# A graph-attention kernel: the first graph's scores taken straight from K and Q

## The chip, the cores and the metric

One core of one Trainium2 chip. The metric is the device time of one execution in microseconds (us), median of several executions.

## The reference

For each of 32 graphs of 256 nodes with 256 features (8 heads of 32), in float32:

```
q, k, v = x @ Wq.T + bq, x @ Wk.T + bk, x @ Wv.T + bv      # split into 8 heads of 32
scores  = q @ k.T * 32**-0.5 * (adj + adj)                 # per head, 256 x 256
attn    = softmax(scores, axis=-1)
ctx     = attn @ v                                         # heads side by side: 256 x 256
out     = layernorm(x + ctx @ Wo.T + bo)
```

## The kernel before

Graphs are worked on singly, but K and Q are projected for a pair of graphs at once (two graphs' 512 nodes are the columns). Every engine runs a loop written out by hand, `step(g)` for g from -4 to 34, with eight places o = 0..7 in it, and does its part of several graphs in a fixed order; semaphores join them. A place o of step g turns head o of graph g (`turn_probs`) and makes the scores three heads ahead (`rows`); three projections of K and Q for a coming pair, the projection of V for the next graph, and the output projection are laid between.

To keep float32 precision with one-pass matmuls, an operand is cut into a high part (rounded) and a low part (the rest), in the type F32R. For the scores, K's and Q's parts of one head, 32 features each, are stacked on 128 rows: four groups of 32 rows hold K high, low, high, low against Q high, high, low, low. So one matmul of 128 rows adds all four products. The way to such a stack is long:

- TensorE projects (`project_kq`, L240; pair 0 uses four banks, later pairs share `proj_bank`, so each projection waits until ScalarE has read the one before);
- ScalarE reads the bank into `whole` and adds the bias (`read_kq`, L477; semaphore `kq_out`);
- GpSimd cuts it into `parts` (`cut_kq`, L538 and L540; `kq_low`);
- 32 copies of 32 x 1024 elements each build `stack` (for K and Q, four pairs of heads, four groups). For all pairs but the first, these are DMAs issued by SyncE (L192), after the DMA that loads the transposed x of the pair after (`xt`, L184, one buffer). For pair 0, SyncE issues 12 of them (K, pairs of heads 0 to 2), VectorE makes 12 and ScalarE 8 by copies (`stack_first`, L145).

VectorE multiplies the scores by the mask `adj_rows` and takes the row maximum in one instruction (`reduce_rows`, L341), ScalarE makes the exponentials (`exp`, L447), TensorE transposes them (L223), VectorE (one head in eight: ScalarE) moves them out, and they multiply V (`weigh_v`, L278). `turn_shares` (L266) spreads the reciprocals of the sums. ScalarE's `cut_x` (L469) takes the high part of `xt`, GpSimd's `low_x` (L546) the low part (`xt_low`). `copy_v` (L481) moves V out. ScalarE also issues the loads of the masks and of x (`load_masks`, `load_x`).

The order of ScalarE around the change, by place: in step -1 `read_kq(1, 0)` at 1, `copy_v(0)` at 3, `read_kq(1, 1)` at 5, `exp(0, 0)` at 7; in step 0 `exp(0, 1)` at 0, `load_masks(1)` and `read_kq(1, 2)` at 1, `load_x(0)` at 2, `copy_v(1)` at 3, then at 4 `exp(0, 5)`, `move_turned`, `cut_x(2, 0)`, at 5 `exp(0, 6)`, `read_kq(1, 3)`, `cut_x(2, 1)`, at 6 `exp(0, 7)`, and at 7 `exp(1, 0)`.

Of the kernel before, what the change touches and what calls it, by code (L numbers as in the profile page):

```python
# [40 lines left out]
def build(nc, x, x_t, adj, adj_t, wq, wk, wv, wo, bq, bk, bv, bo, out):  # L41
    ctx = ExitStack()
    with ctx:
# [83 lines left out]
        def kq_bank(pair, c):  # L127

            return (*row_bank, *turn_bank)[c] if pair == 0 else proj_bank
# [7 lines left out]
            else:  # L137
                wait(eng, moved_dve, (H - len(ON_ACT)) * g + o + 1 - sum(n < o for n in ON_ACT))

        def stack_first(eng, copy, which, j):  # L140

            eng.wait_ge(kq_low, 2 * which + 2)
            for group in range(J):
                part = group % 2 if which == 0 else group // 2
                copy(stack[D * group:D * (group + 1), 0, which, j, :],  # L145
                     parts[D * j:D * (j + 1), 2 * which + part, :]).then_inc(stacked[0][which][j], 16)

        def run_steps(step):
            for g in range(-4, B + 3):
# [2 lines left out]
        def is_graph(g):  # L152
            return 0 <= g < B
# [12 lines left out]
        @block.sync  # L166
        def _(sp):
            sp.dma_start(xt[:].rearrange("p t s -> p (t s)"), x_t[0]).then_inc(xt_in, 16)
            for n, dram in enumerate((wk, wq, wv, wo)):
                sp.dma_start(w_whole[:, n], dram).then_inc(weight_in[n], 16)  # L170
                if n == 0:
                    for tile, bias_dram in ((b_k, bk), (b_q, bq)):
                        sp.dma_start(tile[:], bias_dram).then_inc(biases_in, 16)
            for tile, dram in ((b_v, bv), (b_o, bo)):
                sp.dma_start(tile[:], dram).then_inc(biases_in, 16)

            def step(g):
                if g % 2 == 0 or not is_pair(g + 3):
                    return
                pair = (g + 3) // 2  # L180
                if g + 5 < 2 * PAIRS:

                    wait(sp, xt_low, 2 * pair + 2)
                    sp.dma_start(xt[:].rearrange("p t s -> p (t s)"), x_t[pair + 1]).then_inc(xt_in, 16)  # L184
                for which in range(1 if g == -3 else 2):
                    wait(sp, kq_low, 4 * pair + 2 * which + 2)
                    for j in range(J - 1 if g == -3 else J):

                        wait(sp, rows_made, 8 * g + 2 * j + 2)
                        for group in range(J):  # L190
                            part = group % 2 if which == 0 else group // 2
                            sp.dma_start(stack[D * group:D * (group + 1), pair % 2, which, j, :].bitcast(F32),  # L192
                                         parts[D * j:D * (j + 1), 2 * which + part, :].bitcast(F32)
                                         ).then_inc(stacked[pair % 2][which][j], 16)

            run_steps(step)

        @block.tensor
        def _(pe):
            def rows(n, o):  # L200
                if o % T == 0:
                    for which in range(2):
                        pe.wait_ge(stacked[(n // 2) % 2][which][o // T],
                                   (n // 4) * (J * 16) + J * 16)

                wait(pe, rows_used, 8 * n + o - 1)
                if n == 0 and o == 0:
                    pe.wait_ge(kq_out, 4)
                q, key = head(n // 2, 1, o, n % 2), head(n // 2, 0, o, n % 2)
                for t in range(T):  # L210
                    last = nc.tensor.matmul(row_bank[o % 2][:, t * S:(t + 1) * S], q[:, t * P:(t + 1) * P], key,  # L211
                                            start=(t == 0), stop=True, skip_group_check=True)
                last.then_inc(rows_made, 1)
# [89 lines left out]
                last.then_inc(bias_made, 1)  # L303

            def step(g):
                if g == -2:
                    make_bias()
                for o in range(H):
                    if is_graph(g):
                        turn_probs(g, o)  # L310
                    if o < 5 and is_graph(g):
                        rows(g, o + 3)
                    if o >= 5 and is_graph(g + 1):
                        rows(g + 1, o - 5)
                    if (g % 2, o) in KQ_SLOTS:
                        ahead = kq_ahead(g, o, KQ_SLOTS)
                        if is_pair(g + ahead):
                            project_kq((g + ahead) // 2, *KQ_SLOTS[g % 2, o])
                    if o == 1 and is_graph(g - 1):
                        turn_shares(g - 1, 1)  # L320
                        weigh_v(g - 1, 1)
                    if o == 2 and is_graph(g + 1):
                        project_v(g + 1)
                    if o == 5 and is_graph(g):
                        turn_shares(g, 0)
                        weigh_v(g, 0)
                    if o == 6 and is_graph(g - 1):
                        project_out(g - 1)
# [4 lines left out]
        def _(dve):  # L333
# [56 lines left out]
            for n in range(4):  # L390
# [4 lines left out]
                dve.wait_ge(w_high, n + 1)  # L395
                nc.vector.tensor_tensor(w_parts[:, 1, n].rearrange("p t e -> p (t e)"), tile, high.bitcast(F32),
                                        ALU.subtract).then_inc(w_cut, 1)
            dve.wait_ge(bias_made, 1)
            nc.vector.tensor_copy(bias[:], out_bank[:, 0:E]).then_inc(bias_ready, 1)
            for which, j in ((0, 3), (1, 0), (1, 2)):  # L400
                stack_first(dve, nc.vector.tensor_copy, which, j)

            def step(g):
                for o in range(H):
# [7 lines left out]
                        lower_top(g, o + 2)  # L412
                    if o >= 6 and is_graph(g + 1):
                        lower_top(g + 1, o - 6)
                    if o == 0 and is_graph(g - 1):
                        divide(g - 1, 1)
                    if o in (0, 1) and is_graph(g - 2):
# [15 lines left out]
        def _(act):  # L433
# [37 lines left out]
            def read_kq(pair, c):  # L471
# [2 lines left out]
                if pair == 0 and c == 0:  # L474
                    act.wait_ge(biases_in, 4 * 16)
                b = (b_k if c < 2 else b_q)[:, c % 2:c % 2 + 1]
                nc.scalar.activation(whole[:, c % 2, :], kq_bank(pair, c)[:], ACT.Identity, bias=b).then_inc(kq_out, 1)  # L477

            def copy_v(n):
                act.wait_ge(v_made, n + 1)  # L480
# [11 lines left out]
            nc.scalar.preload_act_table_set("natural_log_exp_and_others")  # L492

            def step(g):
                for o in range(H):
                    if g == -2 and o == 6:
                        stack_first(act, nc.scalar.copy, 1, 1)
                        stack_first(act, nc.scalar.copy, 1, 3)
                    if o < 7 and is_graph(g):
                        exp(g, o + 1)  # L500
                    if o == 7 and is_graph(g + 1):
                        exp(g + 1, 0)
                    if is_graph(g) and o in ON_ACT:
                        move_turned(g, o)
# [24 lines left out]
        def _(pool):  # L529
            def cut_kq(pair, c):  # L530
                cut = slice((c % 2) * 512, (c % 2 + 1) * 512)
                pool.wait_ge(kq_out, 4 * pair + c + 1)
                if c % 2 == 0:

                    if pair > 0:
                        for j in range(J):
                            pool.wait_ge(stacked[(pair - 1) % 2][c // 2][j], ((pair - 1) // 2 + 1) * (J * 16))
                nc.gpsimd.tensor_copy(parts[:, 2 * (c // 2), cut], whole[:, c % 2, :]).then_inc(kq_high, 1)  # L538
                pool.wait_ge(kq_high, 4 * pair + c + 1)
                nc.gpsimd.tensor_tensor(parts[:, 2 * (c // 2) + 1, cut], whole[:, c % 2, :],  # L540
                                        parts[:, 2 * (c // 2), cut].bitcast(F32),
                                        ALU.subtract).then_inc(kq_low, 1)

# [116 lines left out]
```

## Time and profile before

| | us |
|---|---|
| median of 3 executions | 520.39 (519.92 to 523.06) |
| the profiled execution | 522.89 |
| its span, first to last instruction | 521.1 |
| TensorE (PE) busy in it | 472.7, at a mean granted clock of 0.974 |
| VectorE (DVE) busy | 429.8 |
| ScalarE (ACT) busy | 384.0 |
| GpSimd (POOL) busy | 348.7 |

Busy time is the sum over an engine's instructions. The profiled execution carries 1.8 us outside its span. Times in the rows below count from the span's start.

### The profile page before, as it was taken

What the parts mean: (1) busy time and instruction counts of PE and PEld (TensorE: products, weight loads), DVE (VectorE), ACT (ScalarE), POOL (GpSimd) and SP (SyncE); (2) the same over time, 40 slices, a digit from 0 to 9 for tenths busy, and PEclk for the clock granted to TensorE, in tenths of its full rate; (3) what the DMA queues carried; (4) which work ended last, traced back from release to release, by engine and by line L of the source; (5) the groups of instructions that cost most, each with busy time, mean ns of one, the idle gap of its engine ahead of it and who ended that gap; (6) DMA issues with size and microseconds to landing.
All of it is one profiled execution on the core that took longest, in us unless ns stands there. A gap on an engine that the chain in (4) does not pass through costs nothing.

```text
span 521.1 us, 15227 instructions
## 1 busy us (share of the span) xinstructions
PE 472.7 (91%) x4742; PEld 395.2 (76%) x4742; DVE 429.8 (82%) x1815; ACT 384.0 (74%) x1257; POOL 348.7 (67%) x518
## 2 busy tenths in 40 slices
PE   4569999999999999999999999999999999998872
PEld 3357887878788788878888787878888787877752
DVE  4547888888888898888888998988889888888881
ACT  2478887777878777787878777787878777777750
POOL 4724557686876767696876767786776768664444
PEclk9859999999999999999999999999999999999996
DMA  5709897988889798898889897998989889795101
GB/s 161 173 29 240 207 222 176 233 202 205 227 208 240 173 254 193 218 219 206 227 202 235 199 244 173 230 219 205 231 187 260 187 220 214 165 246 128 61 23 41
DMA packets 40322, 100.11 MB, mean 192 GB/s; under 512 B 9649, under 2 KB 17842, under 8 KB 40242
## 3 DMA queue, kind: packets, MB, share of 16 engines
q1 hardware_dynamic: 26930, 73.96, 60.8%
q10 hardware_dynamic: 13312, 25.17, 16.8%
q8 instruction: 39, 0.64, 0.6%
q14 instruction: 41, 0.34, 0.2%
HBM read 26.22 MB, written 8.39 MB: 66 GB/s over the span
## 4 chain that ended last, share of the span: by engine, by line
PE 65%; POOL 21%; issue 5%; DVE 4%; ACT 3%; DMA 1%; POOLq 0%; DVEq 0%; SPq 0%; ACTq 0%
PE turn_bank L223 17%; PE proj_bank L240 11%; PE v_bank L253 9%; PE row_bank L211 8%; PE ctx_bank L278 8%; POOL xt_parts L546 7%; PE ctx_bank L266 5%; PE out_bank L290 5%; POOL parts L540 4%; POOL result L586 3%; POOL ctx_parts L554 2%; POOL scale L573 2%; POOL parts L538 2%; ACT probs L447 2%; POOL ctx_parts L552 1%
## 5 line engine op out<-in xcount | busy, mean ns | idle before, releaser
L447 ACT ACTIVATE probs<-probs,low_top 128x256 f32<-128x256 f32 x512 | 257.6, 505 | 100.9 <-DVE low_top L349 98.4
L356 DVE COPY turned_probs<-turn_bank 128x512 f32<-128x512 f32 x224 | 154.7, 691 | 53.7 <-PE turn_bank L223 52.9
L341 DVE CUSTOM_DVE_ANT_0 probs<-row_bank,adj_rows 128x256 f32<-128x256 f32 x512 | 192.2, 414 | 6.1 <-PE row_bank L211 6.1
L223 PE MATMUL turn_bank<-ident,probs 128*128 128x128 f32 x1024 | 158.2, 277 | 7.8 <-ACT probs L447 7.7
L223 PEld LDWEIGHTS turn_bank<-ident,probs 128*128 128x128 f32 x1024 | 119.5, 141 | 52.1 <-ACT probs L447 23.4
L240 PE MATMUL proj_bank<-xt_parts,w_parts 128*128 128x512 f32 x360 | 107.0, 407 | 21.4 <-POOL xt_parts L546 16.2
L211 PE MATMUL row_bank<-stack 128*128 128x256 f32 x512 | 124.3, 325 | 0.7 <-DVE top L341 0.7
L447 ACT ACTIVATION_READ_ACCUMULATOR probs<-probs,low_top 128x1 f32 x512 | 97.3, 190 | 0.0
L540 POOL TENSOR_TENSOR parts<-whole,parts 128x512 fp32r<-128x512 f32 x64 | 82.9, 1296 | 5.3
L240 PEld LDWEIGHTS proj_bank<-xt_parts,w_parts 128*128 128x128 f32 x360 | 61.0, 193 | 30.8 <-POOL xt_parts L546 19.2
L552 POOL CAST ctx_parts<-context 128x256 fp32r<-128x256 f32 x64 | 25.5, 398 | 86.0 <-DVE context L366 86.0
L211 PEld LDWEIGHTS row_bank<-stack 128*128 128x128 f32 x512 | 78.2, 193 | 1.1 <-issue 0.9
L538 POOL CAST parts<-whole 128x512 fp32r<-128x512 f32 x64 | 39.6, 619 | 50.8 <-ACT whole L477 50.8
L278 PE MATMUL ctx_bank<-turned_probs,v 128*32 128x256 f32 x1024 | 67.0, 379 | 0.0
L290 PE MATMUL out_bank<-w_parts,ctx_parts 128*128 128x256 f32 x384 | 51.7, 285 | 2.2 <-POOL ctx_parts L554 2.2
L253 PE MATMUL v_bank<-w_parts,xt_parts 128*128 128x256 f32 x384 | 52.2, 286 | 0.0
L554 POOL TENSOR_TENSOR ctx_parts<-context,ctx_parts 128x256 fp32r<-128x256 f32 x64 | 47.1, 736 | 5.1
L290 PEld LDWEIGHTS out_bank<-w_parts,ctx_parts 128*128 128x128 f32 x384 | 48.4, 192 | 2.7 <-POOL ctx_parts L554 2.7
L253 PEld LDWEIGHTS v_bank<-w_parts,xt_parts 128*128 128x128 f32 x384 | 49.3, 195 | 0.2
L546 POOL TENSOR_TENSOR xt_parts<-xt,xt_parts 128x512 fp32r<-128x512 f32 x32 | 41.9, 1311 | 7.0 <-ACT xt_parts L469 7.0
L341 DVE DVE_READ_ACCUMULATOR2_ANT top<- 128x1 f32 x512 | 43.4, 85 | 0.0
L266 PE MATMUL ctx_bank<-ident,shares 128*32 128x128 f32 x1024 | 41.2, 278 | 1.6 <-DVE shares L361 1.5
(44 smaller groups left out, 473.0 us busy)
## 6 DMA issues: line engine op xcount, KB each, us to landing
stack<-parts SPq DMA_DIRECT2D x492, 128.0 KB, 2.6
xt<-in_x_t SPq DMA_DIRECT2D x16, 512.0 KB, 3.9
adj_rows<-in_adj ACTq DMA_DIRECT2D x16, 512.0 KB, 4.7
xr<-in_x ACTq DMA_DIRECT2D x16, 512.0 KB, 7.5
out<-result ACTq DMA_DIRECT2D x32, 256.0 KB, 3.2
turned_probs<-in_wk SPq DMA_DIRECT2D x1, 256.0 KB, 4.0
turned_probs<-in_wq SPq DMA_DIRECT2D x1, 256.0 KB, 3.8
turned_probs<-in_wv SPq DMA_DIRECT2D x1, 256.0 KB, 4.0
```

Source lines behind the costliest of these rows:

```text
L211: last = nc.tensor.matmul(row_bank[o % 2][:, t * S:(t + 1) * S], q[:, t * P:(t + 1) * P], key, start=(t == 0), stop=True, skip_group_check ...
L223: last = nc.tensor.transpose(turn_bank[o % 2][:, c * S + t * P:c * S + (t + 1) * P], probs[:, o % RING, t * S + c * P:t * S + (c + 1) * P] ...
L240: last = nc.tensor.matmul(kq_bank(pair, c)[:], w_parts[:, a, c // 2, t, features], xt_parts[:, pair % 2, b, t, :], start=(half_ == 0 and n ...
L253: last = nc.tensor.matmul(v_bank[:, tile * E:(tile + 1) * E], xt_parts[:, (n // 2) % 2, a, t, nodes], w_parts[:, c, 2, t, :], start=(tile ...
L266: nc.tensor.matmul(ctx_bank[c:c + D, S + t * P:S + (t + 1) * P], shares[:, g % 2, o, t:t + 1].to_broadcast([P, D]), ident[:], start=True, ...
L278: last = nc.tensor.matmul(ctx_bank[c:c + D, 0:S], v[:, (g // 2) % 2, g % 2, t, o * D:(o + 1) * D], turned_probs[:, o, t * S:(t + 1) * S], ...
L290: last = nc.tensor.matmul(out_bank[:, n * E:(n + 1) * E], ctx_parts[:, g % 2, a, f, nodes], w_parts[:, b, 3, f, :], start=(n == 0 and i == 0),
L341: last = nc.vector.tensor_tensor_reduce(probs[:, o % RING, t * S:(t + 1) * S], row_bank[o % 2][:, t * S:(t + 1) * S], adj_rows[:, (n // 2) ...
L356: nc.vector.tensor_copy(turned_probs[:, o, :], turn_bank[o % 2][:]).then_inc(moved_dve, 1)
L447: last = nc.scalar.activation(tile, tile, ACT.Exp, bias=low_top[:, n % 2, o, t:t + 1], accum_out=sums[:, n % 2, o, t:t + 1])
L540: nc.gpsimd.tensor_tensor(parts[:, 2 * (c // 2) + 1, cut], whole[:, c % 2, :], parts[:, 2 * (c // 2), cut].bitcast(F32), ALU.subtract).the ...
L546: nc.gpsimd.tensor_tensor(xt_parts[:, pair % 2, 1, t, :], xt[:, t, :], xt_parts[:, pair % 2, 0, t, :].bitcast(F32), ALU.subtract).then_inc ...
```

## The change

Graph 0's scores are no longer made from the stacks, but from K and Q as ScalarE read them out, in float32, each head on its own 32 rows of the array (`rows_of_first`, with `tile_position`). For pair 0 the readouts go to `y` and `result`, which nothing else uses yet (`read_out`), in place of `whole`. Graph 1 still uses pair 0's stacks. All 32 of these are now issued by SyncE; VectorE and ScalarE copy none. TensorE makes graph 0's first three heads of scores at the start of step -1 instead of in its places 5 to 7, followed by the product for the bias (`make_bias`, before at the start of step -2); VectorE copies the bias out at the end of step -1; ScalarE makes the first exponential at the start of step -1 instead of its end.

```diff
--- before.py
+++ after.py
@@ -137,13 +137,11 @@
             else:
                 wait(eng, moved_dve, (H - len(ON_ACT)) * g + o + 1 - sum(n < o for n in ON_ACT))
 
-        def stack_first(eng, copy, which, j):
-
-            eng.wait_ge(kq_low, 2 * which + 2)
-            for group in range(J):
-                part = group % 2 if which == 0 else group // 2
-                copy(stack[D * group:D * (group + 1), 0, which, j, :],
-                     parts[D * j:D * (j + 1), 2 * which + part, :]).then_inc(stacked[0][which][j], 16)
+        def read_out(pair, c):
+
+            if pair == 0:
+                return (y, result)[c // 2][:, c % 2].rearrange("p t e -> p (t e)")
+            return whole[:, c % 2, :]
 
         def run_steps(step):
             for g in range(-4, B + 3):
@@ -182,9 +180,9 @@
 
                     wait(sp, xt_low, 2 * pair + 2)
                     sp.dma_start(xt[:].rearrange("p t s -> p (t s)"), x_t[pair + 1]).then_inc(xt_in, 16)
-                for which in range(1 if g == -3 else 2):
+                for which in range(2):
                     wait(sp, kq_low, 4 * pair + 2 * which + 2)
-                    for j in range(J - 1 if g == -3 else J):
+                    for j in range(J):
 
                         wait(sp, rows_made, 8 * g + 2 * j + 2)
                         for group in range(J):
@@ -197,15 +195,29 @@
 
         @block.tensor
         def _(pe):
+            def rows_of_first(o):
+
+                wait(pe, rows_used, o - 1)
+                if o == 0:
+                    pe.wait_ge(kq_out, 4)
+                j, f = o // T, o % T
+                own = slice(D * j, D * (j + 1))
+                q, key = read_out(0, 2 + f), read_out(0, f)
+                for t in range(T):
+                    last = nc.tensor.matmul(row_bank[o % 2][:, t * S:(t + 1) * S], q[own, t * P:(t + 1) * P], key[own, 0:S],
+                                            start=(t == 0), stop=True, tile_position=(D * j, 0), skip_group_check=True)
+                last.then_inc(rows_made, 1)
+
             def rows(n, o):
+                if n == 0:
+                    rows_of_first(o)
+                    return
                 if o % T == 0:
                     for which in range(2):
                         pe.wait_ge(stacked[(n // 2) % 2][which][o // T],
                                    (n // 4) * (J * 16) + J * 16)
 
                 wait(pe, rows_used, 8 * n + o - 1)
-                if n == 0 and o == 0:
-                    pe.wait_ge(kq_out, 4)
                 q, key = head(n // 2, 1, o, n % 2), head(n // 2, 0, o, n % 2)
                 for t in range(T):
                     last = nc.tensor.matmul(row_bank[o % 2][:, t * S:(t + 1) * S], q[:, t * P:(t + 1) * P], key,
@@ -303,14 +315,16 @@
                 last.then_inc(bias_made, 1)
 
             def step(g):
-                if g == -2:
+                if g == -1:
+                    for o in range(3):
+                        rows(0, o)
                     make_bias()
                 for o in range(H):
                     if is_graph(g):
                         turn_probs(g, o)
                     if o < 5 and is_graph(g):
                         rows(g, o + 3)
-                    if o >= 5 and is_graph(g + 1):
+                    if o >= 5 and 0 < g + 1 < B:
                         rows(g + 1, o - 5)
                     if (g % 2, o) in KQ_SLOTS:
                         ahead = kq_ahead(g, o, KQ_SLOTS)
@@ -395,10 +409,6 @@
                 dve.wait_ge(w_high, n + 1)
                 nc.vector.tensor_tensor(w_parts[:, 1, n].rearrange("p t e -> p (t e)"), tile, high.bitcast(F32),
                                         ALU.subtract).then_inc(w_cut, 1)
-            dve.wait_ge(bias_made, 1)
-            nc.vector.tensor_copy(bias[:], out_bank[:, 0:E]).then_inc(bias_ready, 1)
-            for which, j in ((0, 3), (1, 0), (1, 2)):
-                stack_first(dve, nc.vector.tensor_copy, which, j)
 
             def step(g):
                 for o in range(H):
@@ -412,6 +422,9 @@
                         lower_top(g, o + 2)
                     if o >= 6 and is_graph(g + 1):
                         lower_top(g + 1, o - 6)
+                    if g == -1 and o == 7:
+                        dve.wait_ge(bias_made, 1)
+                        nc.vector.tensor_copy(bias[:], out_bank[:, 0:E]).then_inc(bias_ready, 1)
                     if o == 0 and is_graph(g - 1):
                         divide(g - 1, 1)
                     if o in (0, 1) and is_graph(g - 2):
@@ -474,7 +487,7 @@
                 if pair == 0 and c == 0:
                     act.wait_ge(biases_in, 4 * 16)
                 b = (b_k if c < 2 else b_q)[:, c % 2:c % 2 + 1]
-                nc.scalar.activation(whole[:, c % 2, :], kq_bank(pair, c)[:], ACT.Identity, bias=b).then_inc(kq_out, 1)
+                nc.scalar.activation(read_out(pair, c), kq_bank(pair, c)[:], ACT.Identity, bias=b).then_inc(kq_out, 1)
 
             def copy_v(n):
                 act.wait_ge(v_made, n + 1)
@@ -492,13 +505,12 @@
             nc.scalar.preload_act_table_set("natural_log_exp_and_others")
 
             def step(g):
+                if g == -1:
+                    exp(0, 0)
                 for o in range(H):
-                    if g == -2 and o == 6:
-                        stack_first(act, nc.scalar.copy, 1, 1)
-                        stack_first(act, nc.scalar.copy, 1, 3)
                     if o < 7 and is_graph(g):
                         exp(g, o + 1)
-                    if o == 7 and is_graph(g + 1):
+                    if o == 7 and 0 < g + 1 < B:
                         exp(g + 1, 0)
                     if is_graph(g) and o in ON_ACT:
                         move_turned(g, o)
@@ -535,9 +547,9 @@
                     if pair > 0:
                         for j in range(J):
                             pool.wait_ge(stacked[(pair - 1) % 2][c // 2][j], ((pair - 1) // 2 + 1) * (J * 16))
-                nc.gpsimd.tensor_copy(parts[:, 2 * (c // 2), cut], whole[:, c % 2, :]).then_inc(kq_high, 1)
+                nc.gpsimd.tensor_copy(parts[:, 2 * (c // 2), cut], read_out(pair, c)).then_inc(kq_high, 1)
                 pool.wait_ge(kq_high, 4 * pair + c + 1)
-                nc.gpsimd.tensor_tensor(parts[:, 2 * (c // 2) + 1, cut], whole[:, c % 2, :],
+                nc.gpsimd.tensor_tensor(parts[:, 2 * (c // 2) + 1, cut], read_out(pair, c),
                                         parts[:, 2 * (c // 2), cut].bitcast(F32),
                                         ALU.subtract).then_inc(kq_low, 1)
 
```

## Rows read from the trace of the kernel before

**Rows 1.** Page, busy time by engine: us, share of the span, instructions

```profile
PE 472.7 (91%) x4742; PEld 395.2 (76%) x4742; DVE 429.8 (82%) x1815; ACT 384.0 (74%) x1257; POOL 348.7 (67%) x518
```

**Rows 2.** Windows of one us: engines, granted clock (PEclk), DMA share

```profile
core 0: us, PE busy (x) PEld busy (x) DVE busy (x) ACT busy (x) POOL busy (x), PEclk, DMA share, GB/s
23.00:24.00 1.00, 0.00 (x0) 0.00 (x0) 0.87 (x1) 0.89 (x1) 1.00 (x2) 0.65 0.88 193
...
40.00:41.00 1.00, 1.00 (x6) 0.77 (x6) 1.00 (x5) 0.44 (x2) 0.00 (x0) 0.82 0.98 213
```

**Rows 3.** Timeline of PE, 17 to 72 us: start, length, what

```profile
18.74 0.96 PE L240 MATMUL proj_bank<-xt_parts,w_parts 128*128 128x512 f32 x3 [1.29 <-ACT xt_parts L469]
24.30 1.65 PE L240 MATMUL proj_bank<-xt_parts,w_parts 128*128 128x512 f32 x3 [4.60 <-POOL xt_parts L546]
25.74 2.76 PE L253 MATMUL v_bank<-w_parts,xt_parts 128*128 128x256 f32 x12
32.40 2.93 PE L240 MATMUL proj_bank<-xt_parts,w_parts 128*128 128x512 f32 x6 [3.90 <-ACT whole L477]
...
38.68 1.05 PE L223 MATMUL turn_bank<-ident,probs 128*128 128x128 f32 x4
...
51.96 0.60 PE L223 MATMUL turn_bank<-ident,probs 128*128 128x128 f32 x4
...
61.24 0.48 PE L211 MATMUL row_bank<-stack 128*128 128x256 f32 x2
```

**Rows 4.** Timeline of ACT, 17 to 72 us

```profile
17.49 0.69 ACT L477 ACTIVATE whole<-turn_bank,b_q 128x512 f32<-128x512 f32 x1 [0.16 <-PE turn_bank L240]
...
23.11 8.52 ACT L145 CAST stack<-parts 32x1024 fp32r<-32x1024 f32 x8 [4.43 <-POOL parts L540]
31.66 0.69 ACT L477 ACTIVATE whole<-proj_bank,b_k 128x512 f32<-128x512 f32 x1
...
46.78 0.62 ACT L469 CAST xt_parts<-xt 128x512 fp32r<-128x512 f32 x1
...
50.63 0.52 ACT L447 ACTIVATE probs<-probs,low_top 128x256 f32<-128x256 f32 x1
```

**Rows 5.** Timeline of SP: DMA issues

```profile
15.66 7.57 SPq L192 DMA_DIRECT2D stack<-parts  x12
24.27 0.33 SPq L184 DMA_DIRECT2D xt<-in_x_t  x1
...
38.13 10.54 SPq L192 DMA_DIRECT2D stack<-parts  x16
...
51.02 10.82 SPq L192 DMA_DIRECT2D stack<-parts  x16
```

**Rows 6.** DMA view, windows 40 to 42, 42 to 44, 46 to 49.5 us: KB, us to landing

```profile
adj_rows<-in_adj ACTq DMA_DIRECT2D x1, 512.0 KB, 4.5
...
xr<-in_x ACTq DMA_DIRECT2D x1, 512.0 KB, 7.0
...
stack<-parts SPq DMA_DIRECT2D x4, 128.0 KB, 6.1
```

**Rows 7.** Everything on tile xt: landing of its loads

```profile
DMA to landing us min/median/max: 3.3/3.9/6.2
```

**Rows 8.** Chain of work: start, us on the chain, what

```profile
14.34 1.06 PE out_bank L301 x4
...
54.39 0.24 PE row_bank L211 x2
...
55.20 0.86 PE ctx_bank L278 x16
56.06 0.59 PE turn_bank L223 x4
...
58.31 0.44 PE turn_bank L223 x4
...
58.99 0.69 PE proj_bank L240 x3
```

## Prediction

> **What bounds the kernel now.** I read the busy times first: TensorE is busy 91% of the span [rows 1], so over the 32 graphs it sets the pace, and the kernel's time is the moment at which graph 0 gets under way plus a train of steps that no part of this change touches. Any gain is a shift of that train. I therefore read the start, engine by engine. The end of it is best seen where TensorE transposes the first head of a graph: graph 0's at 38.68 us and graph 1's at 51.96 [rows 3].
>
> What holds graph 0 back: TensorE's work for step -2 ends at 19.70 (18.74 + 0.96), and its next projection waits for the low part of x until 24.30. Then V, until 28.5, and then nothing until 32.40 [rows 3]. The next projection needs `proj_bank` read by ScalarE, and ScalarE copies stacks from 23.11 to 31.63, and reads the bank at 31.66 [rows 4]. Because TensorE idled from 19.70, its granted clock fell between 23 and 24 us and came back only between 40 and 41 [rows 2]: the work of 24.3 to 40.4 went at 1.2 GHz.
>
> **What the change takes away: the start.** Scores of graph 0 need only K and Q read out. The last readout ends at 18.18 [rows 4], before TensorE is free at 19.70. Price of a head in float32: two tiles, each two instructions of 256 columns. The nearest row is `weigh_v`'s, also float32, 256 columns and on a quarter of the array: 16 instructions, four side by side, in 0.86 us, so 0.215 us each when alone; `make_bias` has 4 in 1.06, 0.265 each [rows 8]. A head is thus 0.86 to 1.06 us; I take 0.86, since the first row has the quarter tiles. A head from the stacks took 0.24 [rows 8]. To that comes the change of tiling: the transposes right after `weigh_v` take 0.59 against 0.44 elsewhere, so 0.15 for each change, 0.30 a head. In sum about 1.15 a head, 0.9 more than before.
>
> The Trainium skill, TensorEngine Tiling, section Key Properties, says that changing the tiling mode drains TensorE; the 0.15 us agrees. The skill's TensorE: Matmul & The Clock Gate, Part 3, says that a weight load overlaps matmuls in flight only when its row group differs, and here both tiles of a head have the same one. No row here shows loads on row tiles. By that rule the loads would add to each head, and the sum would be lower by the price given with the rivals.
>
> Heads 0 and 1 take 19.7 to 21.7, head 2 follows when VectorE has used the first bank (masks were issued early and nothing else waits for VectorE then), then `make_bias`, to about 24.2. TensorE's gap is gone, so I expect the clock to stay at 2.4 GHz. From 24.30, at the full clock's prices: 3 instructions of projection 0.69 [rows 8], V 1.43 (12 of 256 columns; half of the 2.76 in rows 3, and what 12 such take at the full clock), two projections 1.4, to 27.8. ScalarE no longer has copies in the way; its readout is 0.69, then one more projection, 29.2. There graph 0's first transpose starts, against 38.68: 9.5 us earlier. VectorE's bias copy, moved behind a wait, has only step 0's work behind it and ends by 25.
>
> **What it adds in step 0.** Five heads (3 to 7) cost TensorE 0.9 more each. Up to head 6's transpose, TensorE does 6 transposes (2.7), 5 float32 heads (5.75), one stack head 0.24, three projections 2.1, V 1.43, `turn_shares` and `weigh_v` with their change of tiling 1.5: 13.7, so it gets there at 42.9. Before, the same place came at 48.8 (38.68 + 10.1). If nothing else bound, the shift would be 5.9 to 6.1.
>
> **What it adds on SyncE, and what is late next.** SyncE issued 12 copies in 7.57 us from 15.66, and 16 in 10.54 and 10.82 later [rows 5]: 0.63 to 0.68 each. Pair 0 now has 32: 15.66 + 32 x 0.655 = 36.6. The second half needs GpSimd's last cut, which was there at 23.1, when ScalarE's copies began [rows 4], and SyncE comes to it only at 26. Behind these 32 stands SyncE's load of `xt` for pair 2, which it issued at 24.27 [rows 5] and will now issue at 36.7. That load takes 3.3 to 6.2 us to land, median 3.9 [rows 7]. Near it are the loads of masks and x, issued by ScalarE with step 0, now about 30.6 and 32.8: before, these took 4.5 and 7.0 us, and a stack copy issued 6 us after the first of them needed 6.1 [rows 6], with a DMA share of 0.98 at 40 us [rows 2]. `xt` is issued exactly 6 us after the masks' load and behind stack copies in the same queue, so it lands at 40.6 to 44; I take 6.2 after 37.0 (its issue done), 43.2.
>
> Who waits: ScalarE's `cut_x(2, 0)`, and behind it in its order head 6's exponential, the readout of Q, `cut_x(2, 1)`, head 7's exponential and graph 1's first. Before, `cut_x(2, 0)` started at 46.78 with ScalarE busy without a pause from there to graph 1's first exponential at 50.63 [rows 4]; TensorE's first transpose of graph 1 was at 51.96. So from this place on the shift is 46.8 minus the landing: 46.8 - 43.2 = 3.6. The ends: landing at 40.6 gives 6.1 by ScalarE, and TensorE's own chain caps it at about 6; landing at 44.1 gives 2.7.
>
> Graph 1's stacks of the first pair of heads land about 31 and are needed at 40. Graph 2's: K's 16 copies from 37.3 to 47.8, then four of Q's to 50.5, landed by 53 to 55 with the queue as full as at 46 us; needed at 61.24 - 3.6 = 57.6 [rows 3, 5]. Covered by 3 us or more; with a shift of 6 it would be even. Later pairs have SyncE pausing for GpSimd, 48.67 to 51.02 in the rows, and the train keeps its shift. The copies saved on VectorE and ScalarE give nothing more: in steps they have no part.
>
> **Sum.** 522.89 - 3.6 = 519.3 for an execution like the profiled one, whose own time is 2.5 above the median of the three. Applied to the median: 520.39 - 3.6 = 516.8.
>
> **Rivals.**
>
> *No stall on xt.* SyncE's issues or the queue run faster, and TensorE binds in step 0. Shift 5.2 to 6.2, time 514.2 to 515.2. For it: the median landing of 3.9 gives 40.9. Against it: that median is taken mostly with no bulk loads ahead. Chance 0.22.
>
> *The early clock falls all the same*, because quarter-array float32 counts for little or the gaps at 17 to 18.7 and 24 do. Then 24.30 to the last projection goes as in rows 3: V ends at 28.5, two projections 31.4, readout 32.1, projection 33.6; step 0 keeps its old slow start and pays the five heads: 5.1 - 4.5 + some 2 of old waits = 2.6, and `xt` is no longer late. Time 517.8. Chance 0.13.
>
> *Weight loads not hidden.* 4 loads a head at some 0.19 add 0.76, five heads 3.8; TensorE would reach head 6 at 46.7, against 44.9 with the late `xt`. Shift 2.1, time 518.3; chance 0.10.
>
> *Slower than before: the wait takes the clock.* With `xt` late, TensorE sits from 42.9 to some 44.9, waiting for head 6's exponential. Before, an idle TensorE lost its clock 3.6 us or a little more after 19.70 [rows 2, 3]. If the landing is at 45 or later, the pause is as long, and the clock can go until some 17 us later as it did the first time; with TensorE's work dense there, up to 8 us are lost. Shift 1.8 - 8 = -6, time up to 526; if the clock returns in 4 us, the loss is 2 and the shift about 0. Chance of a time above before's 0.07; it decides from a landing at 45.
>
> *It doesn't show*: the shift is eaten again later, by stacks of graph 2 that land late or GpSimd's low part of x: 520.4. Chance 0.05.
>
> **Numbers.** My forecast (late `xt`, shift 2.4 to 5.2) has 0.43. The time is 516.8. The range takes in the rival without stall on its fast side (514.2, and 0.7 for the scatter of the medians) and on the slow side shifts down to about 0: 513.5 to 520.8; what lies outside is the clock lost a second time, and parts of the others. One per cent, 5.2 us, is about what a measurement of this kernel can tell from no change. Faster by more than that: the rival without stall and a little of the forecast, 0.25. Within: 0.70. Slower by over 1%: 0.05.
>
> **What the profile after would show.** Heads 0 and 1 at 19.7 on TensorE, four instructions each, some 0.2 apart; the clock at 1.0 from 20 to 40; ScalarE's readout of pair 1 near 25; the first transpose of graph 0 near 29; 32 copies by SyncE to 36.6 and `xt` behind them, a wait of ScalarE for `xt` of 2 to 4 us near 39 to 43, a TensorE wait of some 2 us before head 6; graph 1's first transpose near 48.4, and from there rows like before's, 3.6 earlier. The forecast is wrong if the float32 heads cost much above 1.15 us, if the clock differs, or if `xt` lands outside 41.6 to 44.4.

## The result and the profile after

The changed kernel is slower by about a third of a per cent: 522.54 us median of 18 executions (520.02 to 524.77) against 520.41 of 18 before, ratio 1.0035 with a 95% interval of 1.0021 to 1.0048. I had forecast 516.8, 3.6 us faster. The profiled execution took 523.15 us, its span 521.3 against 521.1. Before's profiled execution lies 2.5 us above its median and the changed kernel's 0.6, so the two profiles differ by 0.3 us where the medians differ by 2.1.

The busy times [rows 1] changed by what was moved: TensorE more, VectorE and ScalarE less by their copies.

```profile
PE 478.7 (92%) x4758; PEld 398.9 (77%) x4758; DVE 420.2 (81%) x1803; ACT 374.6 (72%) x1249; POOL 346.5 (66%) x518
```

The timeline of TensorE after, to be read against [rows 3]. L207 are the float32 heads, L235 the transposes. In the rows below, the number before the engine's name is how long the row took, and brackets hold how long the engine stood idle before it and for what:

```profile
30.39 0.60 PE L235 MATMUL turn_bank<-ident,probs 128*128 128x128 f32 x4
30.92 1.13 PE L207 MATMUL row_bank<-y,result 32*128 32x256 f32 x4
31.98 0.96 PE L252 MATMUL proj_bank<-xt_parts,w_parts 128*128 128x512 f32 x3
...
43.53 1.05 PE L290 MATMUL ctx_bank<-turned_probs,v 128*32 128x256 f32 x16
47.33 1.11 PE L235 MATMUL turn_bank<-ident,probs 128*128 128x128 f32 x4 [2.75 <-ACT probs L460]
...
52.02 1.05 PE L235 MATMUL turn_bank<-ident,probs 128*128 128x128 f32 x4
```

Graph 0's first transpose comes at 30.39, 8.3 us earlier than before's 38.68. Graph 1's first comes at 52.02, where it was 51.96. The whole lead is lost inside step 0. For head 6 the row of before is this:

```profile
48.83 0.66 PE L223 MATMUL turn_bank<-ident,probs 128*128 128x128 f32 x4
```

TensorE after is done with the work ahead of it at 44.58 (43.53 + 1.05), so 4.2 us of the lead are left there: the float32 heads took 4.0, where the forecast gave them 3.6. Then TensorE stands 2.75 us ahead of head 6, and the stretch behind it takes another 1.6. ScalarE's timeline says what it stands for:

```profile
40.56 0.58 ACT L470 COPY turned_probs<-turn_bank 128x512 f32<-128x512 f32 x1 [0.49 <-PE turn_bank L235]
45.66 0.62 ACT L482 CAST xt_parts<-xt 128x512 fp32r<-128x512 f32 x1 [4.52 <-DMA xt<-in_x_t]
46.18 0.51 ACT L460 ACTIVATE probs<-probs,low_top 128x256 f32<-128x256 f32 x1
```

It waits 4.52 us for `xt`. SyncE's timeline, and the DMA view of a window at the load's issue (KB, us to landing):

```profile
16.01 21.02 SPq L190 DMA_DIRECT2D stack<-parts  x32
37.07 0.70 SPq L182 DMA_DIRECT2D xt<-in_x_t  x1
```

```profile
xt<-in_x_t SPq DMA_DIRECT2D x1, 512.0 KB, 8.6
```

The load stands behind the 32 copies, as forecast, and takes 8.6 us, more than any before [rows 7]. The pause also takes the clock, as the windows show (PEclk, the granted clock, is the third number from the right: 0.50 is 1.2 GHz):

```profile
19.00:20.00 1.00, 1.00 (x5) 0.84 (x4) 0.50 (x3) 0.00 (x0) 0.92 (x3) 0.71 0.92 201
44.00:46.00 2.00, 0.58 (x12) 0.10 (x4) 0.38 (x4) 0.34 (x1) 1.35 (x2) 1.00 1.03 232
48.00:50.00 2.00, 1.47 (x8) 1.17 (x7) 1.12 (x4) 2.00 (x8) 1.92 (x3) 0.50 1.05 248
52.00:54.00 2.00, 2.00 (x10) 1.89 (x9) 0.97 (x6) 0.64 (x4) 1.41 (x3) 0.61 0.94 217
```

At 1.2 GHz, head 6 of graph 0 to head 0 of graph 1 takes 4.7 us (47.33 to 52.02) where it took 3.1 (48.83 to 51.96). And there is a wait that I had not foreseen at all, on GpSimd:

```profile
43.48 0.61 POOL L550 CAST parts<-whole 128x512 fp32r<-128x512 f32 x1 [11.52 <-DMA stack<-parts]
...
49.83 1.27 POOL L558 TENSOR_TENSOR xt_parts<-xt,xt_parts 128x512 fp32r<-128x512 f32 x1
```

`cut_kq` may overwrite Q's `parts` only when pair 0's last Q copy has landed. Before, engines had made those copies by 31.6. Now GpSimd stands 11.5 us for them, and behind it in its order stands the low part of `xt`. It is done at 51.10, hidden here behind the later pause.

### The profile page after: what moved, and what is told of

It is laid out like the page before. It is cut to its first block, busy times and chain, and to the rows that moved or that the text cites. A ratio compares the mean times of both kernels' runs of the same rounds, so it can differ in the third digit from the quotient of the medians.

```text
span 521.3 us, 15250 instructions
## 1 busy us (share of the span) xinstructions
PE 478.7 (92%) x4758; PEld 398.9 (77%) x4758; DVE 420.2 (81%) x1803; ACT 374.6 (72%) x1249; POOL 346.5 (66%) x518
## 4 chain that ended last, share of the span: by engine, by line
PE 63%; POOL 21%; issue 4%; SPq 4%; DVE 3%; DMA 2%; ACT 2%; POOLq 0%; DVEq 0%
PE turn_bank L235 16%; PE proj_bank L252 10%; PE v_bank L265 8%; PE ctx_bank L290 8%; PE row_bank L223 8%; POOL xt_parts L558 6%; PE out_bank L302 5%; PE ctx_bank L278 5%; SPq L190 4%; POOL parts L552 3%; POOL result L598 3%; POOL ctx_parts L566 2%; POOL scale L585 2%; DMA xt<-in_x_t 2%; POOL parts L550 2%
## 5 line engine op out<-in xcount | busy, mean ns | idle before, releaser
L235 PE MATMUL turn_bank<-ident,probs 128*128 128x128 f32 x1024 | 159.0, 278 | 9.9 <-ACT probs L460 9.9
L235 PEld LDWEIGHTS turn_bank<-ident,probs 128*128 128x128 f32 x1024 | 120.3, 141 | 54.2 <-ACT probs L460 25.1
L223 PE MATMUL row_bank<-stack 128*128 128x256 f32 x496 | 120.7, 325 | 0.0
L460 ACT ACTIVATION_READ_ACCUMULATOR probs<-probs,low_top 128x1 f32 x512 | 96.1, 188 | 0.0
L552 POOL TENSOR_TENSOR parts<-whole,parts 128x512 fp32r<-128x512 f32 x60 | 77.3, 1289 | 4.9
L223 PEld LDWEIGHTS row_bank<-stack 128*128 128x128 f32 x496 | 75.6, 193 | 0.0
L550 POOL CAST parts<-whole 128x512 fp32r<-128x512 f32 x60 | 36.8, 613 | 50.8 <-ACT whole L490 33.4
L265 PEld LDWEIGHTS v_bank<-w_parts,xt_parts 128*128 128x128 f32 x384 | 48.4, 191 | 0.5 <-issue 0.3
L355 DVE DVE_READ_ACCUMULATOR2_ANT top<- 128x1 f32 x512 | 42.9, 84 | 0.0
```

Of the source, the lines that this page charges most:

```text
L235: last = nc.tensor.transpose(turn_bank[o % 2][:, c * S + t * P:c * S + (t + 1) * P], probs[:, o % RING, t * S + c * P:t * S + (c + 1) * P] ...
L265: last = nc.tensor.matmul(v_bank[:, tile * E:(tile + 1) * E], xt_parts[:, (n // 2) % 2, a, t, nodes], w_parts[:, c, 2, t, :], start=(tile ...
L355: last = nc.vector.tensor_tensor_reduce(probs[:, o % RING, t * S:(t + 1) * S], row_bank[o % 2][:, t * S:(t + 1) * S], adj_rows[:, (n // 2) ...
L460: last = nc.scalar.activation(tile, tile, ACT.Exp, bias=low_top[:, n % 2, o, t:t + 1], accum_out=sums[:, n % 2, o, t:t + 1])
L552: nc.gpsimd.tensor_tensor(parts[:, 2 * (c // 2) + 1, cut], read_out(pair, c), parts[:, 2 * (c // 2), cut].bitcast(F32), ALU.subtract).then ...
```

## The experiments

Each is compared with before in the same session. All start from the changed kernel unless said otherwise.

**Run 1, xt between the halves.** SyncE loads `xt` for pair 2 after K's 16 copies:

```diff
-                if g + 5 < 2 * PAIRS:
+                if g + 5 < 2 * PAIRS and g != -1:
...
                 for which in range(2):
+                    if g == -3 and which == 1:
+                        wait(sp, xt_low, 4)
+                        sp.dma_start(xt[:]..., x_t[2]).then_inc(xt_in, 16)
                     wait(sp, kq_low, 4 * pair + 2 * which + 2)
```

> The changed kernel with one move: SyncE issues the load of xt for pair 2 between pair 0's K and Q stack copies (near 26.5 us) instead of behind all 32 (37.1). My theory: the changed kernel lost its lead because ScalarE stood 4.5 us for this load and TensorE 2.75 us behind it, which also took the clock. The load lands near 31, ScalarE's wait is gone, the clock stays at 2.4 GHz from 27 us on. What is late next is GpSimd: its cut of pair 1's Q waits for all of pair 0's Q copies (until 43.5 in the changed kernel), so its low part of x for pair 2 ends near 49.9 against 52.2 before: graph 1's first transpose 2 to 3.5 us earlier than before's 51.96, time 517.5 to 518.5, ratio to before 0.994 to 0.996. Rival (the float32 heads' cost on TensorE ate the lead): nothing moves, ratio 1.000 to 1.004.

Measured 1.0030 (1.0015 to 1.0045), the ratio that I had given the rival. But the trace is neither's. ScalarE no longer waits for `xt`, and TensorE reaches head 6 at 45.38 without a pause. Then it stops a few instructions later, at the projection for pair 2 in step 1:

```profile
44.92 0.61 POOL L553 CAST parts<-whole 128x512 fp32r<-128x512 f32 x1 [12.47 <-DMA stack<-parts]
...
49.99 1.27 POOL L561 TENSOR_TENSOR xt_parts<-xt,xt_parts 128x512 fp32r<-128x512 f32 x1
```

```profile
48.01 0.66 PE L238 MATMUL turn_bank<-ident,probs 128*128 128x128 f32 x4 [0.36 <-ACT probs L463]
...
51.31 1.27 PE L255 MATMUL proj_bank<-xt_parts,w_parts 128*128 128x512 f32 x3 [2.41 <-POOL xt_parts L561]
52.38 1.06 PE L238 MATMUL turn_bank<-ident,probs 128*128 128x128 f32 x4
```

Graph 1's first transpose is at 48.01, 4 us ahead; its second at 52.38, 1.3 us ahead of before's 53.73, with the clock lost again (1.06 us for what takes 0.60). I had seen GpSimd as the next limit, but priced it 1.4 us too early (49.9) and its pause without its clock. The profiled execution, 521.83 us, is 1.2 us below the median of its kernel and before's is 2.5 above its own, which is how these rows can show a lead of 1.3 us where the ratio shows a loss.

**Run 2, both waits removed.** As run 1, and pair 0's cut of Q goes to `ctx_parts`, unused until the end of step 0, where `cut_context(0, 0)` waits for the copies:

```diff
...
+        q_first = ctx_parts[:]...rearrange("p (w n) -> p w n", w=2)
+        def cut_of(pair, n):
+            return q_first[:, n - 2] if pair == 0 and n >= 2 else parts[:, n]
...
-                    if pair > 0:
+                    if pair > 0 and (pair, c) != (1, 2):
                         for j in range(J):
```

> As the run with xt between the halves, and pair 0's cut of Q goes to its own place (the still unused tile of the context's parts), so that GpSimd needn't wait for pair 0's Q copies before it cuts pair 1's Q. If GpSimd's wait is what is late next, as I expect, graph 1's first transpose comes near 47.7 (TensorE's own chain: 44.6 when it reaches head 6, and 3.1 more), time 516 to 516.5, ratio 0.991 to 0.993, and GpSimd's low part of x is done before 47. If that wait doesn't bind, the time is that of the run without this part.

Measured 0.9923 (0.9900 to 0.9945), 517.34 us: some 6 us below the changed kernel by the ratios, 4 below before. TensorE's timeline:

```profile
43.87 0.66 PE L243 MATMUL turn_bank<-ident,probs 128*128 128x128 f32 x4
...
46.50 0.66 PE L243 MATMUL turn_bank<-ident,probs 128*128 128x128 f32 x4 [0.36 <-ACT probs L468]
46.91 0.48 PE L231 MATMUL row_bank<-stack 128*128 128x256 f32 x2
47.23 0.86 PE L260 MATMUL proj_bank<-xt_parts,w_parts 128*128 128x512 f32 x3
48.18 0.66 PE L243 MATMUL turn_bank<-ident,probs 128*128 128x128 f32 x4
```

Graph 1 starts at 46.50, 5.5 ahead, and no pause follows.

**Run 3, a filler in the pause.** Twelve matmuls into a free bank ahead of head 6; the wait for `xt` stays:

```diff
+                    if g == 0 and o == 6:
+                        pe.wait_ge(bias_ready, 1)
+                        for _ in range(12):
+                            nc.tensor.matmul(out_bank[:], w_parts[:, 0, 0, 0, 0:P], xt_parts[:, 1, 0, 0, :], ...)
```

> The changed kernel with 12 extra matmuls of 128x512 in F32R (2.6 us, into a bank that nobody reads then) ahead of graph 0's head 6 transposes, where TensorE otherwise stands 2.75 us. The wait for xt stays, only TensorE's idleness goes. If the clock that fell at 47.4 us was lost by that pause, it stays at 2.4 GHz and head 6 of graph 0 to head 0 of graph 1 takes 3.1 us as in the kernel before instead of 4.7: 1.5 to 2 us faster than the changed kernel, ratio to before 0.999 to 1.001. If the clock falls for another reason or costs nothing, the ratio stays at 1.003.

Measured 0.9996 (0.9983 to 1.0009), 2 us below the changed kernel's ratio. `xt` took 8.7 us, as in the changed kernel (8.6). The granted clock of 48 to 52 us is 1.00, and head 6 to graph 1's head 0 takes 2.9 us:

```profile
48.35 0.60 PE L235 MATMUL turn_bank<-ident,probs 128*128 128x128 f32 x4
...
51.25 0.60 PE L235 MATMUL turn_bank<-ident,probs 128*128 128x128 f32 x4
```

From ScalarE's `cut_x(2, 0)` to graph 1's first transpose it is 5.2 us (46.06 to 51.25), as in before (46.78 to 51.96), and 6.4 in the changed kernel (45.66 to 52.02). So the lost clock was worth 1.2 us at that place, 1.5 at graph 1's second transpose and 2 by the ratios, about the size of the slowdown.

**Run 4, the float32 heads alone.** Pair 0's stacks are again made by DMA, VectorE and ScalarE, 12, 12 and 8 copies. ScalarE's stand behind its first exponential now, and 8 of VectorE's behind the bias copy.

> The float32 heads alone: pair 0's stacks are made as before, 12 by DMA, 12 by VectorE (8 of them after the bias copy), 8 by ScalarE after its first exponential; the rest as in the changed kernel. xt is issued near 24 as before, nobody waits for it, GpSimd is not held. ScalarE's copies hold its readout of pair 1 again until near 31, so graph 0's first transpose is near 36. TensorE pays 5 x 0.9 us for the float32 heads of step 0. My sum: 2.5 us from the start, minus up to 4.5 less the 1 to 2 us that TensorE waited for ScalarE in that step before: graph 1's first transpose 0 to 1.5 us later than before, ratio 1.000 to 1.003. If the stacks by DMA are what cost (rival), it is faster than the changed kernel by 2 us or more.

Measured 1.0112 (1.0074 to 1.0150), but with times spread from 523 to 536 us, which no theory had and which makes the ratio worth little. I ran it again:

> The float32 heads with pair 0's stacks by the engines once more, because its times lay between 523 and 536 and its profile had the clock at 1.2 GHz from 33 to 63 us with TensorE busy all through graph 0's step. If it is a matter of when the clock is lost, a faster execution (523) shows the clock back before 45 us; if the float32 heads always hold it down, this profile shows 1.2 GHz until head 7 is made.

Measured 1.0055 (1.0036 to 1.0073). The clock was back at 36 us, so the heads do not always hold it down; the first profile, of the slowest execution (536.13 us), had it at 1.2 GHz from 33 to 63 us with TensorE busy nearly all the time. TensorE's timeline of the second shows the heads' plain price:

```profile
37.03 0.60 PE L243 MATMUL turn_bank<-ident,probs 128*128 128x128 f32 x4
...
53.77 0.66 PE L243 MATMUL turn_bank<-ident,probs 128*128 128x128 f32 x4 [0.36 <-ACT probs L472]
```

Step 0 lasts 16.7 us against 13.3 before, at an early start of only 1.7. With the copies back on the engines the kernel is no faster than the changed one, since ScalarE's copies hold the start again. This run can't say what the DMA copies cost, because it trades one cost for another; runs 1, 2 and 6 do. What it shows is that the copies had to leave ScalarE for the heads to pay.

**Run 5, the other half alone.** The kernel before, its heads from the stacks, with all 32 copies by DMA and both repairs of run 2.

> The kernel before with only its second half changed: pair 0's stacks all by DMA, none by engines, xt for pair 2 loaded between K's and Q's copies, pair 0's cut of Q in its own place; graph 0's heads still come from the stacks. Q's first four copies land near 31.5, so head 0 of graph 0 is made near 31.5 and its transposes start near 34 instead of 38.7; the later heads' stacks follow at 2.7 us for two heads and more with the bulk loads in the queue, which may stall heads 6 and 7 by up to 3 us. If the gain of the run with both repairs (0.992) came from taking the copies off ScalarE, this one is at 0.990 to 0.996 without any float32 head; if the float32 heads are what pays, it is at 0.998 or above.

Measured 0.9982 (0.9971 to 0.9994), on the boundary that I had set for "the float32 heads are what pays". TensorE:

```profile
26.72 1.53 PE L240 MATMUL proj_bank<-xt_parts,w_parts 128*128 128x512 f32 x6
33.02 1.12 PE L211 MATMUL row_bank<-stack 128*128 128x256 f32 x4 [4.76 <-issue]
35.20 0.76 PE L211 MATMUL row_bank<-stack 128*128 128x256 f32 x2 [1.07 <-DMA stack<-ctx_parts]
```

With the copies off the engines the projections are done at 28, but the stacks come 5 us later, and the clock is at 1.2 GHz from 36 to 38 us. The float32 heads fill just this time. Against run 2 they are worth 0.6%, 3 us. Neither half pays by itself: this one gains 0.2%, run 4's loses over 0.5%.

**Run 6, only GpSimd's wait removed.** Run 2 without run 1's move.

> The changed kernel with only pair 0's cut of Q in its own place, so that GpSimd isn't held, and xt still behind the 32 copies. If ScalarE's wait for xt alone is enough to lose the lead (my theory, two waits each enough by itself), xt lands near 45.6 as before and the ratio is 1.001 to 1.004; if GpSimd's wait was the one that counted, it is 0.992 to 0.996.

Measured 1.0021 (1.0005 to 1.0037). `xt` took 9.3 us, ScalarE waited 5.3 and TensorE 3.55 ahead of head 6, at 48.14. With runs 1 and 2 this makes the square of the two repairs: with neither 1.0035, with one or the other 1.0030 and 1.0021, with both 0.9923. There are two waits, and each is enough by itself.

**Run 7, a filler at the start.** Run 2 with six matmuls ahead of the first projection of pair 1:

```diff
+                    if pair == 1 and half_ == 0:
+                        for _ in range(6):
+                            nc.tensor.matmul(v_bank[:], w_parts[:, 0, 0, 0, 0:P], xt_parts[:, 0, 0, 0, :], ...)
```

> The run with both repairs, and 6 extra F32R matmuls of 128x512 (1.3 us, into a bank not yet in use) in TensorE's pause ahead of its first projection for pair 1 (15.3 to 16.7 us). If the clock that fell near 19 us in the middle of the float32 heads was lost by that pause, it stays at 2.4 GHz and graph 0's first transpose comes 1 to 1.5 us earlier (28.5): ratio 0.989 to 0.991. If the float32 heads on a quarter of the array lose it themselves, it falls near 19 all the same and the ratio stays at 0.992.

Measured 0.9896 (0.9872 to 0.9920), 516.00 us. The windows show the clock at 1.00 all through the float32 heads, and the first transpose is at 27.40, where run 2 has it at 29.77:

```profile
18.00:20.00 2.00, 1.98 (x9) 1.39 (x8) 0.73 (x4) 0.00 (x0) 1.92 (x3) 1.00 0.95 209
20.00:22.00 2.00, 1.90 (x10) 1.37 (x10) 1.04 (x8) 1.09 (x4) 1.98 (x2) 1.00 0.93 201
```

```profile
27.40 0.60 PE L243 MATMUL turn_bank<-ident,probs 128*128 128x128 f32 x4
...
54.89 0.47 PE L231 MATMUL row_bank<-stack 128*128 128x256 f32 x2 [1.32 <-issue]
```

The last timeline row is graph 2's first head, waiting for its stack: the copies are late there too. The prediction had them even "with a shift of 6"; here graph 1's first transpose (44.12) is 7.8 us ahead. The intervals of runs 2 and 7 overlap, so for the time the gain of the filler is likely, not settled; the clock and the earlier start are seen in the rows.

**Run 8, fewer DMA copies.** Run 7 with the last pair of heads' 8 copies by VectorE.

> Both repairs and the early filler, and the last pair of heads' 8 copies of pair 0 (4 of K, 4 of Q) made by VectorE in pauses that it has (11 to 19 us and after the bias copy) instead of by DMA. With all 32 as DMAs, TensorE's first head of graph 2 waited 1.3 us near 54.9 for its stack, the 36th and later copies in the queue. Eight copies less bring that 5.3 us forward: the wait goes, ratio 0.986 to 0.989. If it stays at 0.990, the stacks' queue was not what is late there; if VectorE's copies delay the first maxima, graph 0's first transpose comes later than 27.4.

Measured 0.9943 (0.9930 to 0.9957), a miss. VectorE:

```profile
15.46 5.37 DVE L156 CAST stack<-parts 32x1024 fp32r<-32x1024 f32 x4 [3.88 <-POOL parts L575]
20.86 0.42 DVE L375 CUSTOM_DVE_ANT_0 probs<-row_bank,adj_rows 128x256 f32<-128x256 f32 x1
```

Its four copies of K took 5.37 us where the four of Q later took 3.14. They held the first maxima, TensorE stood 2.1 us for a bank and lost its clock there (0.79 for 20 to 21 us, then 0.50), and graph 0's first transpose came at 31.67, 4.3 us after run 7's. The pause that I gave VectorE was not wide enough.

**Run 9, one bulk load out of the way.** The changed kernel with `load_masks(1)` in place 6 of step 0 instead of place 1.

> The changed kernel with one load moved: the masks for pair 1 (512 KB) are issued in place 6 of step 0 instead of place 1, so they are not in flight ahead of xt. xt landed 8.6 us after its issue, 2.4 more than the 6.2 I had priced. If the bulk loads ahead of it made the difference, it lands in 6 to 7 us (44 or earlier), ScalarE's wait shrinks from 4.5 to about 3, TensorE's pause from 2.75 to 1 to 2, the clock may stay, ratio 0.996 to 1.000, GpSimd's low part of x for pair 2 (49.9 at the earliest) being the next limit. If the 32 copies in its own queue make it, it stays at 8 us or more and the ratio at 1.002 to 1.004.

Measured 0.9942 (0.9929 to 0.9954), better than its range. In this run `xt` landed in 6.0 us, at 43.4 where I had forecast 43.2, and graph 1 starts at 48.57 where I had 48.4:

```profile
43.40 0.62 ACT L482 CAST xt_parts<-xt 128x512 fp32r<-128x512 f32 x1 [1.76 <-DMA xt<-in_x_t]
```

```profile
47.15 0.66 PE L235 MATMUL turn_bank<-ident,probs 128*128 128x128 f32 x4 [1.18 <-ACT probs L460]
47.88 0.86 PE L252 MATMUL proj_bank<-xt_parts,w_parts 128*128 128x512 f32 x3
48.57 0.60 PE L235 MATMUL turn_bank<-ident,probs 128*128 128x128 f32 x4
49.25 0.86 PE L252 MATMUL proj_bank<-xt_parts,w_parts 128*128 128x512 f32 x3
```

The shift is 3.4 in these rows and 3.0 by the ratio, and the clock stays. TensorE's pause is shorter than forecast, 1.18 us, and stands ahead of head 7. Pair 0's Q copies also landed earlier (GpSimd goes on at 41.69 instead of 43.48), so GpSimd's low part was done at 48.88, just ahead of the projection at 49.25: the one move shortened both waits.

**Run 10, all that helped.** Run 7 and run 9's move.

> All that helped together: xt between the halves, pair 0's cut of Q in its own place, the early filler, and the masks for pair 1 loaded in place 6 instead of 1. The masks' load is out of the way of pair 0's last copies and pair 1's first, so TensorE's wait of 1.3 us for graph 2's first stack should shrink or go: ratio 0.987 to 0.990 against 0.990 without this last part. If the masks then come late for graph 2, VectorE waits for them near 50 us and it is above 0.990.

Measured 0.9910 (0.9884 to 0.9935): not told apart from run 7. TensorE's wait for graph 2's stack was 1.02 us instead of 1.32. Both are about 1% faster than before and more than that against the changed kernel. That wait for the queue is the longest that TensorE has left in this stretch; what it is worth was not tried apart.

## Why the prediction was wrong

- *The start.* 29.2 was forecast for the first transpose, 30.39 measured. Two errors partly cancel in this, which is luck. The clock fell at 19 us, which I had as a rival (0.13); by runs 2 and 7 (29.77 and 27.40) that costs 2.4 us. And with the clock kept the chain is 1.8 us shorter than forecast (27.40), because TensorE starts the heads at 18.22 and not at 19.7: the product for the bias, which had been ahead of them, was itself moved. The sequence, and ScalarE free for the readout (at 25.72), were as forecast.
- *The float32 heads.* Forecast 1.15 us with both changes of tiling. Measured 1.06 from the head to the next instruction (30.92 to 31.98) and 0.17 more on the transposes before it (0.53 to the next start, against 0.36): 1.23. The 1.06 is the upper end of my range, `make_bias`'s 0.265 for each instruction, where I had taken `weigh_v`'s 0.215. TensorE's own chain for step 0, 13.7 forecast, was some 14.2 (30.39 to the end of `weigh_v` near 44.6). The rival of unhidden weight loads is out: four loads at 0.19 would have made the 1.06 at least 1.6. So the sentence of the Trainium skill (TensorE: Matmul & The Clock Gate, Part 3) that I had set against the sum was not borne out here. The Trainium skill's TensorEngine Tiling, Key Properties, states that a change of tiling mode drains TensorE; the 0.17 agrees.
- *SyncE.* 32 copies to 36.6 forecast, 37.03 measured.
- **The step that failed: "it lands at 40.6 to 44; I take 6.2 after 37.0, 43.2".** It took 8.6 and ScalarE went on at 45.66. I had used the longest landing of any `xt` load before, though before, at 24.27 and 61.88, that load was issued with no bulk load of ScalarE's just ahead of it. Runs 3 and 6, with the same loads in flight, had 8.7 and 9.3. Run 9 shows the term: without the masks' load in flight it took 6.0, and the kernel did what I forecast (3.4 against 3.6). So the mechanism, a shift of 46.8 less the landing, held where the clock stayed, and the landing was mis-sized by 2.4 us. By that formula the landing takes 2.5 of the 3.6 us and leaves 1.1.
- *What hangs on it.* The rival "the wait takes the clock", "decides from a landing at 45", had 0.07. It is what happened, at 45.66, with a pause of 2.75 us. The sum had put this term at nothing. It took what was left: the shift at graph 1's first transpose is 51.96 - 52.02, none. The rival's price was up to 8 us, or 2 if the clock returns in 4 us; run 3 puts it at 1.5 to 2. I took for its condition a pause of 3.6 us, from the one case in the rows. That was too sure: 2.75 was enough. TensorE came to head 6 at 44.6 and not at 42.9, or the pause would have been longer still.
- *The shift was taken off the median.* "Applied to the median: 520.39 - 3.6" uses a shift read from an execution 2.5 us above it. In the profiled execution the forecast missed by 3.9 us (519.3 against 523.15), in the median by 5.7 (516.8 against 522.54). The other executions of before say why this matters: of the 29 measured beside runs 1 to 4, eight took 522.2 to 523.5 us at a mean granted clock of 0.971 to 0.976, the rest 520.5 to 521.8 at 0.978 to 0.984. The profile (522.89, 0.974) is one of the former. I take it that most executions of before lose less to the clock than [rows 2] show, so that part of what the change takes away was not there to take. That is argued, not shown: how their start looks was not profiled.
- *What was left out.* I had followed the copies into SyncE's queue and to their readers, but not to the engine that waits for their end in order to reuse their source, GpSimd's `cut_kq`. The wait stands in its code. It costs nothing in the changed kernel, where ScalarE is later still, but run 1 shows that it alone is enough to lose most of the lead, and my rival "no stall on xt" (shift 5.2 to 6.2, chance 0.22) could not have come true for it.
- *What stays open.* The changed kernel's 18 executions spread over 4.8 us, the 12 of run 3 over 1.0. That fits a landing and a clock that differ from one to the next, but only one was profiled. Whether the masks' load delays `xt` by its bytes, by its place in a queue or otherwise was not taken apart. Why run 4 spread to 536 wasn't settled either.

## What to carry to other kernels

When copies move from engines to a DMA queue, follow three parties: who is next in the queue, who waits for what is next, and who waits for the copies' source to come free. An early start is kept only if all three move with it; here there were two waits, removing either one showed almost nothing, and removing both brought 6 us. Where a load crosses bulk transfers of another queue, take no landing time from rows in which no such transfer was in flight, and look at what an in-order engine has behind that wait, the clock of TensorE included. And before a shift read from one profile is taken off a median, see where that execution lies among the others.

## What the runs showed of the hardware

- TensorE's clock fell from 2.4 to 1.2 GHz in a pause of 2.75 us, where I had expected to need 3.6, and within 1 us after a pause of 2.41 in run 1 (0.50 for 52 to 54 us); it stayed through one of 1.18 in run 9. It also fell at 19 us, while float32 heads on a quarter of the array kept TensorE busy, after a pause of 1.4 us ahead of them. With six full matmuls in that pause (run 7) it stayed at 2.4 GHz through the same heads.
- A float32 head of four instructions of 256 columns on a quarter of the array took 1.06 us at 2.4 GHz, the same as `make_bias`'s four on the whole array [rows 8]. Its four weight loads (0.185 us each in the median) hardly showed. At 1.2 GHz it took 2.00 (run 4's first profile), where the clock stayed down for 30 us of busy TensorE; in its second, the same program had it back within 4 us of TensorE's restart at 32.5.
- The 512 KB load of `xt` took 3.3 to 6.2 us before, 8.6 to 9.3 behind 32 copies with masks and x in flight (changed kernel, runs 3 and 6), and 6.0 with the masks' load moved away (run 9).
- VectorE's copies of 32 x 1024 took 1.3 us each at 15 to 21 us and 0.8 at 26 to 29, in run 8.
